# Mixture-of-experts layer on one core: another order of the first loads, and one empty product less

## What is computed

```python
g = jnp.einsum('bsd,edf->ebsf', h, Wg)
u = jnp.einsum('bsd,edf->ebsf', h, Wu)
expert_outs = jnp.einsum('ebsf,efd->ebsd', jax.nn.silu(g) * u, Wd)
expert_output = jnp.einsum('be,ebsd->bsd', gating_probs, expert_outs)
shared = jnp.einsum('bsf,fd->bsd', jax.nn.silu(h @ Sg) * (h @ Su), Sd)
return (1.0 - sg) * expert_output + sg * shared      # the caller adds x
```

## Time and profile before

| | |
|---|---|
| time, median of 3 runs | 156.63 us (156.59 to 157.03) |
| the profiled execution, its time | 156.61 us |
| its span, first to last instruction | 155.3 us |
| TensorE (PE) busy | 152.2 us, 98% of the span |
| ScalarE, VectorE, GpSimd busy | 108.9, 98.6, 77.4 us |
| granted TensorE clock, mean of the core | 1.000 |

### The profile page before, as it was taken

How to read it: one execution, slowest core, us unless ns; L and a number is a source line. 1 busy time by engine, 2 the same in 40 slices (tenths; PEclk the granted TensorE clock), 3 DMA queues, 4 the chain that set the end, 5 groups by cost and what they waited for, 6 DMA issues and landing times.

```text
span 155.3 us, 2306 instructions
## 1 busy us (share of the span) xinstructions
PE 152.2 (98%) x673; PEld 124.3 (80%) x673; DVE 98.6 (63%) x160; ACT 108.9 (70%) x204; POOL 77.4 (50%) x78
## 2 busy tenths in 40 slices
PE   7999999999999999999999999999999999999993
PEld 2888888888888888888888888888888888888873
DVE  0597677765666666666666666666665666666692
ACT  4877876776687757775778577766776687755541
POOL 1758993547255645546354825572547255650000
PEclk9999999999999999999999999999999999999999
DMA  4975015004100330005000500070000000000006
GB/s 145 254 177 176 0 21 186 0 2 168 36 0 0 101 108 0 0 27 175 0 0 0 203 0 0 0 186 16 0 0 0 0 0 0 0 0 4 0 0 135
DMA packets 12727, 8.24 MB, mean 53 GB/s; under 512 B 5041, under 2 KB 10673, under 8 KB 12721
## 3 DMA queue, kind: packets, MB, share of 16 engines
q1 hardware_dynamic: 12144, 7.64, 17.8%
q10 hardware_dynamic: 576, 0.52, 1.0%
HBM read 7.64 MB, written 0.52 MB: 53 GB/s over the span
## 4 chain that ended last, share of the span: by engine, by line
PE 98%; ACT 0%; issue 0%
PE y_ps L519 10%; PE y_ps L521 10%; PE y_ps L528 10%; PE u_ps L639 9%; PE g_ps L634 9%; PE g_ps L635 9%; PE u_ps L640 9%; PE u_ps L641 9%; PE g_ps L636 9%; PE u_ps L507 2%; PE u_ps L600 1%; PE g_ps L588 1%; PE g_ps L591 1%; PE u_ps L602 1%; PE u_ps L599 1%; PE g_ps L586 1%
## 5 line engine op out<-in xcount | busy, mean ns | idle before, releaser
L431 DVE TENSOR_TENSOR h_ps<-silu,u_ps 128x512 f32<-128x512 f32 x71 | 49.2, 696 | 49.0 <-PE u_ps L641 44.6
L345 ACT ACTIVATE h_hi<-h_ps 128x512 fp32r<-128x512 f32 x71 | 42.5, 599 | 38.3 <-DVE h_ps L431 38.3
L251 POOL TENSOR_TENSOR w_lo<-w_raw,w_hi 128x384 fp32r<-128x384 f32 x32 | 32.5, 1016 | 38.3 <-ACT w_hi L335 38.2
L436 DVE TENSOR_TENSOR h_lo<-h_ps,h_hi 128x512 fp32r<-128x512 f32 x71 | 48.4, 683 | 0.1
L340 ACT ACTIVATE silu<-g_ps 128x512 f32<-128x512 f32 x72 | 42.8, 597 | 0.2 <-PE g_ps L565 0.2
L256 POOL TENSOR_TENSOR xs_lo<-xs,xs_hi 128x512 fp32r<-128x512 f32 x16 | 20.6, 1290 | 15.8 <-ACT xs_hi L331 15.8
L528 PE MATMUL y_ps<-h_lo,w_hi 128*128 128x512 f32 x71 | 27.6, 389 | 0.0
L521 PE MATMUL y_ps<-h_hi,w_hi 128*128 128x512 f32 x71 | 27.6, 389 | 0.0
L519 PE MATMUL y_ps<-h_hi,w_lo 128*128 128x512 f32 x71 | 27.6, 389 | 0.0
L634 PE MATMUL g_ps<-x_hi,w_hi 128*128 128x512 f32 x64 | 24.9, 389 | 0.0
L635 PE MATMUL g_ps<-x_lo,w_hi 128*128 128x512 f32 x64 | 24.9, 389 | 0.0
(11 more groups left out here) (81 smaller groups left out, 118.7 us busy)
## 6 DMA issues: line engine op xcount, KB each, us to landing
w_raw<-in_L_cond_Wg SPq DMA_DIRECT2D x8, 256.0 KB, 2.9
w_raw<-in_L_cond_Wu SPq DMA_DIRECT2D x8, 256.0 KB, 3.4
w_raw<-in_L_cond_Wd SPq DMA_DIRECT2D x8, 256.0 KB, 3.8
x_nat<-in_x SPq DMA_DIRECT2D x2, 128.0 KB, 2.9
w_raw<-in_L_cond_Su ACTq DMA_DIRECT2D x2, 128.0 KB, 3.4
w_raw<-in_L_cond_Sd SPq DMA_DIRECT2D x1, 256.0 KB, 4.1
x_blk<-in_x SPq DMA_DIRECT2D x4, 64.0 KB, 3.1
out<-y_blk SPq DMA_DIRECT2D x4, 64.0 KB, 2.2
```

What stands on the lines that cost most here:

```text
L345: act.activation(h_hi[k % HB][:, :], h_ps[k % BANKS][:, :], ACT.Copy)\
L431: dve.tensor_tensor((to or h_ps[k % BANKS])[:, :], silu[k % BANKS][:, :], u_ps[k % BANKS][:, :], ALU.mult).then_inc(hidden_done, 1)
L436: dve.tensor_tensor(h_lo[k % HB][:, :], h_ps[k % BANKS][:, :], f32(h_hi[k % HB][:, :]), ALU.subtract).then_inc(h_lo_done, 1)
```

## The change

The three pieces of the tokens now have a load and a semaphore each. SP loads piece 0 (block 0, 64 KB) and then piece 2 (blocks 2 and 3, 128 KB); ScalarE loads piece 1 (block 1, 64 KB) ahead of the gate slices 0 and 1. The up slices 2 and 3 go from ScalarE's queue to SP's, behind the gate slices 2 and 3. VectorE rounds block 1 as well as block 0, where ScalarE did it before. One empty product of 512 columns is left out ahead of the transposes.

```diff
-WARM_UP = 6
+WARM_UP = 5
...
+        def load_piece(queue, i):
+            some = slice(*PIECES[i])
+            queue.dma_start(x_nat[:, some, :], x_view[0][:, some, :]).then_inc(first_x_loaded[i], DMA)
+
         def sync_program(sp):
-            def load_tokens(i):
-                some = slice(i * HALF_Q, (i + 1) * HALF_Q)
-                sp.dma_start(x_nat[:, some, :], x_view[0][:, some, :]).then_inc(first_x_loaded[i], DMA)
-
-            load_tokens(0)
-            load_tokens(1)
+            load_piece(sp, 0)
+            load_piece(sp, 2)
             load_slices(sp, GATE, Sg, 1)
+            load_slices(sp, UP, Su, 1)
             sp.dma_start(w_raw[0][:, DOWN, :, :], in_rows(Sd)).then_inc(first_down_loaded, DMA)
...
         def scalar_program(act):
+            load_piece(act, 1)
             load_slices(act, GATE, Sg, 0)
             load_slices(act, UP, Su, 0)
-            load_slices(act, UP, Su, 1)
...
-            act.wait_ge(x_transposed, 2)
-            act.activation(x_hi[:, 0, P:HALF_N], first_ps[1][:, 0:P], ACT.Copy).then_inc(x_hi_done[0], 1)
             first_hi(UP, 0, 2)
...
             dve.tensor_copy(x_hi[:, 0, 0:P], first_ps[0][:, 0:P]).then_inc(x_hi_done[0], 1)
+            dve.wait_ge(x_transposed, 2)
+            dve.tensor_copy(x_hi[:, 0, P:HALF_N], first_ps[1][:, 0:P]).then_inc(x_hi_done[0], 1)
...
             def transpose_piece(i):
                 n, m = PIECES[i]
+                pe.wait_ge(first_x_loaded[i], DMA)
...
-            pe.wait_ge(first_x_loaded[0], DMA)
             transpose_piece(0)
             transpose_piece(1)
             for _ in range(WARM_BETWEEN):
                 warm(HALF_N)
-            pe.wait_ge(first_x_loaded[1], DMA)
             transpose_piece(2)
```

More of the change, by code:

```diff
@@ L101, in build @@
         nat_ps = [g_ps[1], u_ps[0], y_ps[0]]
-        first_x_loaded = [sem(f"first_x_loaded{i}") for i in range(2)]
+        first_x_loaded = [sem(f"first_x_loaded{i}") for i in range(len(PIECES))]
         second_x_loaded = sem("second_x_loaded")
```

## The result

The changed kernel takes 157.41 us (median of 22 executions, 156.74 to 159.15), the kernel before 156.63 (22 executions, 156.30 to 157.15). The ratio is 1.0073, with a 95% interval of 1.0046 to 1.0099: slower, by less than 1%. The means of the executions give the same 1.0073, the two medians 1.0050. The median hides what happened. Twelve executions lie between 156.74 and 157.45 (median 157.1), ten, the late ones, between 158.36 and 159.15, and none between. The ratios leave out executions over 1.5% above the fastest of their kernel as slow ones: here 159.15 (granted clock 0.989, so nine late ones of 21 remain), and one late execution each in e3 (159.11), e8 (158.96) and e9 (159.22), all at a clock of 1.000. The kernel before has one group. The profiled execution of the changed kernel is one of the late ones, 158.87 us with a span of 157.6.

What follows compares the result with a forecast made beforehand. TensorE was taken to bound the kernel, its full pace set by C. The transposes' possible -0.22 us is not taken and C moves by +0.21: the profiled 156.61 plus 0.21 is 156.82, forecast 156.8 us, range 156.3 to 157.4.

Steps and rivals of the forecast that it cites:

- C: Start of ScalarE's copy of blocks 2 and 3, 5.01 us before; claimed to set the full pace, forecast at 5.22.
- full pace: TensorE's 512-column products at 0.23 us each, from 6.03 us; shifts of its start were to move the end one for one.
- step of the pace: TensorE's rise from 1.2 to 2.4 GHz in the opening, read near 5.1 us in the profile before.
- Up slices third: In ScalarE's queue: their load lands at 4.87 us, and C, behind their rounding, moves by +0.21 us.
- The term of +0.21: Forecast delay of C in us, from 5.01 to 5.22, passed on to the kernel's time.
- Smaller first token loads: On both queues: block 0 lands at 3.4 us instead of 3.55, and the last transposes could start 0.22 us earlier.
- the bound of 3.2: Earliest landing in us allowed for block 0, from 128 KB less in flight, worth 0.37 us.
- Gate slices second: In ScalarE's queue: they land at 4.06 us, the first real product starts at 4.59, 0.20 earlier, ahead of C.
- VectorE rounds block 1: One more cast on VectorE, 0.20 us, hidden by the gate slices' later arrival; otherwise up to 0.20 on the first products.
- What was to shift behind: One more SP load, 0.43 us, ahead of expert 0's down weights, out of 0.92 us of slack: no cost.
- TensorE stays slow: Rival, chance 0.10: TensorE in the opening steps up late, 0.47 us per us of delay, up to 2.0, giving 158.8.
- One empty product less: Ahead of the transposes: the empty products end at about 3.1 us instead of 3.55, by itself worth nothing.

Runs made afterwards that it cites:

- e3: The changed kernel with ScalarE copying blocks 2 and 3 before it rounds the up slices, five empty products; 156.92 us.
- e8: e7 without the empty product between the second and third piece; 156.77 us, ratio 1.0011.
- e9: The changed kernel with three short empty products instead of one between the second and third piece, five ahead; 157.09 us, ratio 1.0025.
- e1: The changed kernel with six empty products ahead instead of five; 157.06 us, ratio 1.0029.
- e7: The kernel before with VectorE rounding block 1 as well, old loads and six empty products kept; 156.58 us, ratio 1.0006.
- e11: e8 with one empty product of 128 columns added behind the last transposes; 156.88 us, ratio 1.0005.
- e4: e3 with six empty products ahead instead of five; 156.70 us, ratio 1.0011.
- e6: The changed kernel with four empty products ahead instead of five; 158.28 us, ratio 1.0114.
- e10: The kernel before, old loads, with four empty products ahead instead of six; 157.82 us, ratio 1.0062.
- e2: The kernel before, old loads, with five empty products ahead instead of six; 157.03 us, ratio 1.0024.
- e5: The changed kernel with two more 256-column empty products, behind the last transposes and ahead of the gate products of columns 256 to 511; 157.05 us, ratio 1.0055.

## Why the prediction was wrong

**The bound was right.** TensorE ends the kernel, and e1 shows C, full pace and end moving by 0.43, 0.40 and 0.38. But C sets the full pace only where nothing else comes later: in e3 it was the gate slices' load, in e7 and e11 the step of the pace, in e8 TensorE's own products.

**"Up slices third" was right in mechanism and too small in size.** The landing was put at 4.87, halfway between two neighbours; it was 4.97 in the changed kernel and 1.67 + 3.4 = 5.07 in e1. C was put at 5.22 and was 5.32 and 5.44. The term of +0.21 measures +0.31 in the changed kernel's trace, and +0.47 as the difference of the early group to the kernel before (157.1 to 156.63), +0.53 in e1. Alone it would have stayed in the range: e1 lies at 157.06.

**"Smaller first token loads"** brought more than was allowed: block 0 landed at 2.94, below the bound of 3.2, for its load took 2.2 us from issue to landing instead of 2.8, 0.6 less and not the 0.37 that the rate alone says. It changed nothing, since C waited for the up slices. "Gate slices second" came out in the changed kernel's trace (first product at 4.59, as forecast), but not in e3, e4 and e6 (5.23, 5.24 and 4.99). "VectorE rounds block 1" costs nothing (e7), even with the old loads, where the prediction allowed it up to 0.20. What was to shift behind (expert 0's weights) shifted without a cost.

**The step that failed** is the weight of the rival "TensorE stays slow", given 0.10 with the words "the idle is short beside what was fed", and with it the term "One empty product less", which the sum puts at nothing ("By itself this is worth nothing"). The rival's mechanism and its price were right: it was priced at 2.0 us and 158.8 for a low stretch of another 4.3 us, and the profiled execution took 158.87 with the step near 10.1, some 4.4 us after the second half's start. That length was supposed there and not worked out, so that it fits is partly luck. But it happened in 10 of 22 executions and not in one of ten. Against e1 the missing empty product adds 0.35 us to the median and 0.7 to the mean. The median of such a pair of groups lies wherever the halfway mark falls. It fell between the two highest of the twelve early executions, at 157.41, which is 0.01 above the range; with one more late execution it would have been near 157.9. The forecast treated the empty products by where they stand in the chain, where they cost and hide nothing; their use here was to keep TensorE at work. The rule of the Trainium skill that was weighed (TensorE: Matmul & The Clock Gate, Part 1, What's actually happening: the lower level is the default, activity lifts it) agrees with the late shares here: 0 of 12 in e1 with six empty products, 5 of 6 in e6 and 4 of 7 in e10 with four. That the transposes do not count as activity in the same way (its Part 4) no run here separates.

What stays open: why the same five empty products give a group at 158.8 with the new loads and none with the old ones (e2), though TensorE pauses longer ahead of its first transposes there; the pauses lie differently. e5 (3 late of 12) and e9 (1 of 12) hint that the pauses before 4 us matter more than those after, on numbers too small to show it. It is also open how much the late share of one kernel differs from one occasion to the next, as the changed kernel was not run again beside the experiments. And e2's shift of 0.5 us has one late load to show for it in one trace.

## What to carry to other kernels

Empty products that keep TensorE fed until its pace steps up can set the time even when a load hides them: taking one away must be judged over many executions, by their groups, since a single trace or a median of three can show either. When loads are reordered, look behind the load that moves back for in-order work that has nothing to do with it; here a copy of the tokens stood behind the rounding of the up slices, and the tokens' earlier landing was lost there. An opening that starts earlier in one trace need not end earlier: in e8 0.31 us at the full pace were 0.19 at the end. No version tried beats the kernel before beyond what the measurement can tell; e4, e7, e8 and e11 are level with it.

## What was unexpected of the hardware

The moment of the step moves from execution to execution: about 5.1 us in the earlier trace rows, 6.35 in e7, 6.6 in e11, 8.2 in e10, 10.1 in the changed kernel, all from products that began at 0.78. The granted clock in the profile read 1.00 throughout. The same load in the same place of the queue also varies: the gate slices in the second place took 2.9 us from issue to landing in the changed kernel and 3.6 in e4, and those in the third place of SP's queue 3.4 us in one execution and 4.9 in another (the kernel before and e2, whose loads are the same), enough to stop TensorE 8 us into the kernel.
